# Rotating one tile of keys and queries on VectorE instead of GpSimd, and two small steps of a norm with it, in a two-layer attention and experts kernel

## The reference

```python
x = x + _L0_attn_ref(_layernorm(x, axis=-1), ...)
x = x + _L0_ffn_ref(_layernorm(x, axis=-1), ...)      # 16 experts, top 2
x = x + _L1_attn_ref(_layernorm(x, axis=-1), ...)
x = x + _L1_ffn_ref(_layernorm(x, axis=-1), ...)      # 32 experts, top 8
```

```python
def apply_rotary(t, pos, scale):
    return t * jnp.cos(pos) * scale + rotate_half(t) * jnp.sin(pos) * scale
...
attn = jnp.einsum('bnih,bjh->bnij', q, k)
attn = jnp.where(causal, -jnp.finfo(attn.dtype).max, attn)
attn = jax.nn.softmax(attn, axis=-1)
out = jnp.einsum('bnij,bjd->bind', attn, v)
out = out @ w_proj.T + b_proj
```

## Time and profile before

| | |
|---|---|
| median of 3 runs | 1125.06 us (1124.02 to 1129.27) |
| the profiled execution | 1130.29 us |
| its span, first to last instruction | 1128.6 us |
| PE busy | 889.0 us (79%) |
| DVE busy | 687.4 us (61%) |
| ACT busy | 467.2 us (41%) |
| POOL busy | 632.6 us (56%) |
| mean granted TensorE clock | 0.849 |

### The profile page before, as it was taken

How to read it: one execution, slowest core, us unless ns; L and a number is a source line. 1 busy time by engine, 2 the same in 40 slices (tenths; PEclk the granted TensorE clock), 3 DMA queues, 4 the chain that set the end, 5 groups by cost and what they waited for, 6 DMA issues and landing times.

```text
span 1128.6 us, 22056 instructions
## 1 busy us (share of the span) xinstructions
PE 889.0 (79%) x5927; PEld 689.5 (61%) x5927; DVE 687.4 (61%) x2668; ACT 467.2 (41%) x1176; POOL 632.6 (56%) x878
## 2 busy tenths in 40 slices
PE   1578888888597899268888788997599999999900
PEld 0456666665554788156666556564488888888700
DVE  5688898774553355366788666354255555555578
ACT  2336566554310344145665444331144444444400
POOL 3646666533137356375558888877366665665600
PEclk9769899897889899556989877598699999999955
DMA  7600000000253553700001222277555555555287
GB/s 214 225 1 1 1 2 1 1 2 2 80 225 109 149 151 104 261 0 1 2 1 72 83 94 100 100 246 293 200 173 175 179 177 174 175 171 169 69 355 314
DMA packets 72965, 136.97 MB, mean 121 GB/s; under 512 B 13278, under 2 KB 51597, under 8 KB 70800
## 3 DMA queue, kind: packets, MB, share of 16 engines
q1 hardware_dynamic: 52016, 85.15, 23.3%
q0 software_dynamic: 17632, 46.73, 11.6%
q10 hardware_dynamic: 3200, 3.70, 0.9%
HBM read 79.15 MB, written 62.39 MB: 125 GB/s over the span
## 4 chain that ended last, share of the span: by engine, by line
PE 32%; POOL 11%; DVE 8%; issue 5%; DMA 2%; ACT 1%; POOLq 0%; DVEq 0%; SPq 0%; ACTq 0%
PE s_psum L2047 12%; POOL rows L1577 7%; PE s_psum L2060 6%; PE s_psum L2039 3%; DVE f_rows L2148 2%; DVE f_xT L2148 2%; DVE a_masked L1089 2%; PE s_psum L2055 2%; POOL a_probs L1436 1%; PE s_psum L649 1%; DMA rows<-f_rows,f_place_at 1%; PE s_psum L552 1%; PE s_psum L605 1%; PE s_psum L585 1%; PE s_psum L632 1%
## 5 line engine op out<-in xcount | busy, mean ns | idle before, releaser
L2159 POOL DMA_INDIRECT parts<-e_y,e_dest x206 | 202.6, 984 | 154.8 <-issue 121.6
L2047 PE MATMUL s_psum<-wres,e_xT 128*128 x824 | 215.1, 384 | 0.3 <-ACT e_xT L2088 0.2
L1436 POOL TENSOR_SCALAR_AFFINE_SELECT a_probs<-a_probs 128x256 f32<-128x256 f32 x256 | 108.7, 449 | 120.1 <-ACT a_probs L873 119.6
L2047 PEld LDWEIGHTS s_psum<-wres,e_xT 128*128 128x128 f32 x824 | 158.1, 193 | 22.6 <-issue 1.1
L1577 POOL DMA_INDIRECT rows<-f_rows,f_place_at x128 | 125.3, 979 | 36.3 <-issue 32.3
L873 ACT ACTIVATE a_probs<-s_psum 128x768 f32<-128x768 f32 x128 | 104.6, 817 | 75.2 <-PE s_psum L632 73.5
L2093 ACT ACTIVATE e_act_out<-s_psum 128x128 f32<-128x128 f32 x206 | 57.2, 278 | 178.1 <-PE s_psum L2047 178.1
L2122 DVE TENSOR_TENSOR e_hid<-e_act_out,s_psum 128x128 f32<-128x128 f32 x206 | 59.5, 289 | 113.2 <-PE s_psum L2055 84.2
L2060 PE MATMUL s_psum<-wres,e_hT 128*128 x412 | 123.6, 382 | 0.0
L1089 DVE CUSTOM_DVE_ANT_0 a_masked<-s_psum,a_ahead 128x128 f32<-128x128 f32 (+1 forms) x256 | 76.0, 353 | 42.7 <-PE s_psum L608 42.2
L2131 DVE TENSOR_SCALAR e_y<-s_psum,e_xg 128x256 f32<-128x256 f32 x206 | 99.7, 484 | 1.0 <-issue 1.0
(11 more groups left out here) (299 smaller groups left out, 1993.1 us busy)
## 6 DMA issues: line engine op xcount, KB each, us to landing
e_xg<-rows SPq DMA_DIRECT2D x159, 160.0 KB, 2.3
f_rows<-parts SPq DMA_DIRECT2D x8, 1024.0 KB, 7.3
f_xT<-parts SPq DMA_DIRECT2D x8, 1024.0 KB, 7.8
wres<-in_experts SPq DMA_DIRECT2D x21, 384.0 KB, 5.7
e_xg<-rows SPq DMA_DIRECT2D x47, 144.0 KB, 2.2
wres<-in_experts SPq DMA_DIRECT2D x4, 1536.0 KB
rows<-empty SPq DMA_DIRECT2D x1, 5120.0 KB, 24.5
parts<-e_y,e_dest POOLq DMA_INDIRECT x206, 2.4
```

Of the source, the lines that this page charges most:

```text
L1436: last = nc.gpsimd.affine_select(out=diagonal[:, :, a], in_=diagonal[:, :, a], compare_op=ALU.is_ge, fill=0.0, base=0, pattern=[[0, 2], [1 ...
L2047: last = nc.tensor.matmul(ps_u[b % 2][:, 0:2 * P], xT[b % 2][:, c * P:(c + 1) * P], wres[:, ds(e, 1), 2 * c * P:2 * (c + 1) * P].rearrange ...
L2159: nc.gpsimd.indirect_dma_start(out=parts[:, :], out_offset=bass.IndirectOffsetOnAxis(ap=dest[b % NY][:], axis=0), in_=y[b % NY][:], in_off ...
```

## The change

For the last two batches, 6 and 7, the rotation is split. GpSimd keeps the first tile: products in slot 4, sum in slot 5, now in `turn_first`. VectorE takes the second tile whole, in `turn_second`, in slot 7 of rounds 4 and 5, behind `stack_maxima` and ahead of `route_eligible`. Batches 0 to 5 stay as they were. For all eight batches, VectorE computes the front norm's negated mean and variance plus epsilon right behind the aggregate of its statistics, and GpSimd keeps the power and the last product.

```diff
@@ front_stats, VectorE
                 for t in range(TB):
                     last = nc.vector.bn_aggr(f_mv[:, t], f_stats[:, t])
-                last.then_inc(f_var_ready, 1)
+                dve_f.inc(last)
+                dve_f.wait(dve)
+                nc.vector.tensor_scalar(f_neg_mean[:], f_mv[:, :, 0], -1.0, None, ALU.mult)
+                nc.vector.tensor_scalar(f_var_eps[:], f_mv[:, :, 1], LN_EPS, None, ALU.add).then_inc(f_var_ready, 1)
...
+            def turn_second(s):
+                dve_late_rot.start(s - shared_turns)
+                dve.wait_ge(raw_done, TB * (s + 1))
+                dve_late_rot.inc(nc.vector.tensor_tensor(rot_c[:, 1], qk_raw[:, 1], tab_c[:, 1], ALU.mult))
+                half = HD // 2
+                for a, b in ((0, half), (half, 0)):
+                    last = nc.vector.tensor_tensor(all_heads(rot_s, 1)[:, :, a:a + half],
+                                                   all_heads(qk_raw, 1)[:, :, b:b + half],
+                                                   all_heads(tab_s, 1)[:, :, a:a + half], ALU.mult)
+                dve_late_rot.inc(last)
+                dve_late_rot.wait(dve)
+                dve.wait_ge(rot_done, TB * s + 1)
+                wait(dve, stack_lo, TB * s)
+                nc.vector.tensor_tensor(rotated[:, 1], rot_c[:, 1], rot_s[:, 1], ALU.add).then_inc(rot_done, 1)
...
                     if j == 7 and live(i + 2):
                         rms_first(i + 2)
+                    if j == 7 and live(i + 2) and i + 2 >= shared_turns:
+                        turn_second(i + 2)
...
@@ front_rstd, GpSimd
-                pool_f.inc(nc.gpsimd.tensor_scalar(f_var_eps[:], f_mv[:, :, 1], LN_EPS, None, ALU.add))
-                pool_f.wait(pool)
-                nc.gpsimd.tensor_scalar(f_neg_mean[:], f_mv[:, :, 0], -1.0, None, ALU.mult)
...
-                    if live(i + 2):
+                    if live(i + 2) and i + 2 >= shared_turns and j in (4, 5):
+                        turn_first(i + 2, j == 4)
+                    if live(i + 2) and i + 2 < shared_turns:
                         if j == 4:
                             pool_rot.start(i + 2)
                             turn_cos(i + 2, 0)
```

More of the change, by code:

```diff
@@ L476, in attention @@
         pool_ln = Chain(sem("pool_ln"), 2)
-        pool_f = Chain(sem("pool_f"), 2)
-        dve_f = Chain(sem("dve_f"), 1)
+        pool_f = Chain(sem("pool_f"), 1)
+        dve_f = Chain(sem("dve_f"), 2)
         dve_route = Chain(sem("dve_route"), 1000)
@@ L482, in attention @@
         pool_rot = Chain(sem("pool_rot"), 2 * TB)
+        pool_late_rot = Chain(sem("pool_late_rot") if front is not None else None, 2)
+        dve_late_rot = Chain(sem("dve_late_rot") if front is not None else None, 2)
+        shared_turns = B if front is None else B - 2
         def turn_free(eng, name, s):
@@ L1419, in turn_sum, with turn_first @@
                                         ALU.add).then_inc(rot_done, 1)
+            def turn_first(s, first_half):
+                if first_half:
+                    pool_late_rot.start(s - shared_turns)
+                    pool.wait_ge(raw_done, TB * s + 1)
+                    passed(pool, waited_pool)
+                    pool_late_rot.inc(nc.gpsimd.tensor_tensor(rot_c[:, 0], qk_raw[:, 0], tab_c[:, 0], ALU.mult))
+                    half = HD // 2
+                    for a, b in ((0, half), (half, 0)):
+                        last = nc.gpsimd.tensor_tensor(all_heads(rot_s, 0)[:, :, a:a + half],
+                                                       all_heads(qk_raw, 0)[:, :, b:b + half],
+                                                       all_heads(tab_s, 0)[:, :, a:a + half], ALU.mult)
+                    pool_late_rot.inc(last)
+                    return
+                wait(pool, stack_lo, TB * (s - 1) + 1)
+                pool_late_rot.wait(pool)
+                nc.gpsimd.tensor_tensor(rotated[:, 0], rot_c[:, 0], rot_s[:, 0], ALU.add).then_inc(rot_done, 1)
             def moe_rstd(first, end):
```

## The result

The changed kernel took 1118.61 us (median of 20 runs, 1114.68 to 1127.98) against 1124.77 us (median of 20, 1120.15 to 1137.05) for the kernel before, measured beside it. The ratio is 0.996, with a 95% interval of 0.9943 to 0.9978: 4.5 us faster, between 2.5 and 6.4; the medians lie 6.2 us apart. The forecast was 4.9 us and 1120.2.

What follows compares the result with a forecast made beforehand. GpSimd was taken to bound from 594 us to the experts, with TensorE nearly level. TensorE's gain of 3.9 us through round 8 plus 1.0 in the tail made -4.9: 1120.2 us from 1125.06, range 1117.3 to 1123.5.

Steps and rivals of the forecast that it cites:

- GpSimd bounds from the first scatter to the experts: Second attention stage: GpSimd hardly ever stops for another engine from 594 us to the experts, 200 us of the span.
- 7.8 us leave GpSimd: GpSimd's own work saved: 4.7 us of second-tile rotations in two rounds, 3.1 us of norm operations in rounds 5 to 10.
- The ports, 1.1 us: GpSimd's maskings and scatters lose 1.1 us beside VectorE's two rotations, between 0 and 1.6.
- VectorE's rotation, 1.5 us: Rounds 4 and 5, ahead of the routing: each second-tile rotation takes VectorE 1.5 us, between 1.2 and 2.0.
- The norm pair: Front norm's two small operations on VectorE, with their wait for the aggregate: some 0.3 us, charged to TensorE in round 5.
- TensorE's lateness: TensorE against before: +1.8 us at turn 4 to 5, +1.1 at turn 5 to 6, then -2.05 and -2.3.
- Rounds 6 and 7 hold -2.3: TensorE stays 2.3 us earlier through rounds 6 and 7, VectorE having no rotation there; round 8 makes it 3.9.
- rival 1: GpSimd's saving of 6.7 to 7.8 us arrives whole if TensorE's slow stretches shrink: 1118.4 to 1117.3 us; chance 25%.
- its own sign: Sign that the forecast is right: GpSimd shows waits for exponentials in rounds 6 to 8.
- The tail, -1.0: After round 8 GpSimd bounds alone; two more pairs of norm operations leave it, 1.0 us.

Runs made afterwards that it cites:

- rotation behind the routing: The changed kernel with VectorE's rotation after the routing (`route_chosen`) instead of ahead of it; 1123.4 us against 1127.33 for the kernel before.
- left out: The changed kernel without the second tile's rotation of batches 6 and 7 on either engine; 1121.97 us against 1125.8 for the kernel before.
- in slot 1: The changed kernel with VectorE's rotation in slot 1 of the next round instead of slot 7; 1124.26 us against 1125.8 for the kernel before.
- shift on ScalarE (2nd): Second run of the changed kernel with the front norm's last product also moved, to ScalarE; 1123.54 us against 1127.01 for the kernel before.
- second trace of the changed kernel: Trace of the changed kernel run again without edit; 1120.94 us against 1127.33 for the kernel before.
- rotation only: The changed kernel with the front norm's two operations back on GpSimd; second run, on a slow chip, 1162.93 us against 1164.94 for the kernel before.

## Why the prediction was right, step by step

- **GpSimd bounds from the first scatter to the experts**: shown where it hardly waits, and only there. Work added to VectorE alone cost 0.3 us of the stretch, each half of GpSimd's relief shortened it by 4.0 to 5.2 us, both by 7.6 and 8.5. But four other kernels relieve GpSimd by as much or more and differ in what VectorE or ScalarE does: rotation behind the routing, left out, in slot 1, and shift on ScalarE (2nd). Their stretches are 7.0, 4.8, 4.6 and 3.6 us shorter than before's, and GpSimd waited 3.1, 6.1, 5.6 and 9.2 us for exponentials in them. How much of the relief arrives goes with how long GpSimd waits for exponentials. (The stretch is 213 us long, not the 200 of the prediction.)
- **7.8 us leave GpSimd**: right. Its rotation fell by half, the norm pairs were 1.4 and 1.4 us of work with 0.9 of idle, 3.7 where I had 3.1.
- **The ports, 1.1 us**: mis-sized. The scatters and maskings that stay cost 0.3 us less in sum, not more. Beside the second rotation one scatter took 1.12 us in place of 0.98; beside the first, none was longer. It was VectorE's sum that stretched there, 0.68 us where the second took 0.44. The rows of 0.99 and 1.49 from which I took the term, belong to a_stack's subtraction, and the changed kernel still shows such a scatter. Beside that subtraction, which began first decides:

```profile
616.45 0.69 DVE L1080 TENSOR_TENSOR a_stack<-a_rotated,a_stack 128x512 fp32r<-128x512 f32 x1
616.57 1.40 POOL L1616 DMA_INDIRECT rows<-f_rows,f_place_at  x1 [0.31 <-issue]
...
644.91 0.98 POOL L1616 DMA_INDIRECT rows<-f_rows,f_place_at  x1 [0.17 <-issue]
645.29 0.69 DVE L1080 TENSOR_TENSOR a_stack<-a_rotated,a_stack 128x512 fp32r<-128x512 f32 x1
```

  The scatter behind the subtraction's start took 1.40 us, the one ahead of it 0.98. Behind the start of one of the rotation's shorter operations it was 1.12 us at 630.93 and 0.96 at 602.29, so these cost little or nothing. By the rule of the Trainium skill that I had weighed ("SBUF — State Buffer", "Who interferes with whom"), the loss was to be 0.3 to 0.4 us; the trace is nearer to that than to my 1.1. Beside the subtraction it agrees that whoever starts first matters, but not that a scatter is spared, unless a scatter counts as reading SBUF.
- **VectorE's rotation, 1.5 us**: 1.52 us in the first place, 1.28 in the second (630.77 to 632.05); the way from the stacked maxima to a_chosen_r grew from 2.25 to 3.75 and 3.82 us. The norm pair, forecast at 0.3, shows as 0.17 and 0.16 us, 0.08 apart.
- **TensorE's lateness**: measured from the first scatter, its scores were 1.3 us later after the first turn (I had 1.8) and 1.1 after the second (I had 1.1). Its products were 2.3 us earlier at the place of 645.30 (I had 2.05), and 2.6 at that of 653.20 (2.3). So far within 0.5 us: VectorE did take GpSimd's place at the turns, and the forecast had this part right.
- **"Rounds 6 and 7 hold -2.3"**: this is the term of the sum that was off. At the places of 700.70 and 714.20 us the changed kernel has these:

```profile
691.26 1.08 PE L652 MATMUL s_psum<-a_probs,a_v 128*32 128x256 f32 x8
...
702.37 0.64 PE L652 MATMUL s_psum<-a_probs,a_v 128*32 128x256 f32 x8 [0.21 <-POOL a_probs L1473]
```

  The gains are 3.7 and 6.1 us, where I had 2.3 and 3.9. The last of these products takes 0.64 us where at 714.20 it took 1.08. What differs there is the clock. These are the three windows of before that answer to the last three of the changed kernel above; the granted clock is the third number from the end, 0.85, 0.71 and 0.59 against 0.82, 0.82 and 0.83:

```profile
656.63:674.63 18.00, 14.22 (x128) 10.46 (x128) 12.06 (x71) 8.20 (x14) 15.27 (x22) 0.85 0.28 102
674.63:694.63 20.00, 19.54 (x158) 14.07 (x158) 13.34 (x76) 8.24 (x13) 16.96 (x28) 0.71 0.26 92
694.63:725.63 31.00, 26.89 (x175) 18.14 (x177) 13.23 (x66) 11.13 (x18) 26.29 (x41) 0.59 0.27 98
```

  TensorE had room, and GpSimd's last masking came 6.2 us earlier, not 3.9. This is rival 1's time up to here, and its mechanism of a shorter slow stretch. That the clock is the cause is read from these windows, and no run could set it. It isn't the last window alone: the second trace of the changed kernel has 0.82, 0.90 and 0.67 in the three and gained 6.3 us. Nor was rival 1 right whole: by its sign GpSimd was to wait for nothing, and it waited 2.2 us for exponentials in rounds 6 and 7, which the forecast had named as its own sign (its sum left room for 1.7).
- **The tail, -1.0**: -1.4 in the first trace and -2.3 in the second, against one trace of before.

In the stretch where the change works the gain was thus 7.6 to 8.5 us, at the upper end of rival 1 (6.7 to 7.8) or a little above it, not 4.9. The whole time moved by 5.2 us (both comparisons together), what the forecast gave. What lies between is the rest of the program, and I can't settle it: over the traces here the second stage starts between 458.2 and 469.9 us with no edited line ahead of it; three of the four that came there by 461.1 us then took 130.7 us to the first scatter, all others 126.9 to 128.4, so that some of an early start is given back. Whether the change's full 7.6 us reach the mean of many executions, or a part is lost in those in which TensorE's slow stretch lasts longer, one trace for each run doesn't show. So the nearness of the forecast's number is partly luck: its turns were right, but its ports were too dear and its TensorE too slow behind them, which made it smaller than the stretch's gain, and the whole time's gain is smaller too for a reason that isn't known.

## What to carry to other kernels

Find the engine that never waits, and charge a change first for what it takes from or gives to that engine: 3 us of new work on VectorE cost 0.3 us of the stretch, 7.8 us off GpSimd brought 7.6. Then look whether the engine still never waits: where exponentials came late, the same relief brought only 4.6 to 4.8. A wait that vanishes on a follower (TensorE's 7 us for maskings) is no gain by itself, since it comes back under another name. And cut both traces at the same events before you compare them: here the spans differ by 13 us, of which 7.6 lie where the change works. One trace of each kernel isn't enough either: where a stretch was traced twice without a disturbance, it moved by up to 1 us, and before against itself by 2.9 us in the whole.

## What the runs showed of the hardware

- TensorE's slow stretch behind the first scatter comes in every trace at the same place, and its length differs between kernels that differ by a few operations: a granted clock of 0.51 to 0.60 in the window from 45 to 62 us and the upper level for most of the next in eleven traces, 0.50 to 0.58 in both in three, two of them of one kernel on two chips. In these three GpSimd waited 6.1 to 11.5 us for exponentials, against 2.2 in the changed kernel. Such waits also came without it, 5.6 us with the rotation in slot 1 and 6.1 us in the second trace of rotation only.
- The same kernel took 1165 us on one of the chips and 1125 to 1127 us on the others, with a mean clock of 0.848 against 0.849 in the profiled executions. In the last rounds the difference lies in standstills of several us that name no partner ("remote"). What they are the traces don't say, and where the 22 us in the experts come from wasn't followed.
- The four operations of a rotation took 1.52 and 1.28 us on VectorE and 2.34 us on GpSimd.
- A scatter issued on GpSimd took 0.98 us alone. Where it began 0.07 to 0.16 us behind VectorE's 128x512 subtraction, it took 1.38 to 1.49 us (seven traces), 0.4 to 0.5 us behind 1.11 to 1.28; where it had begun first, 0.96 to 1.07 us.
